# Second attention layer: other sequences of work in the VectorE and TensorE queues of one head

## The reference, cut to what matters

```python
scores = jnp.einsum('bhqd,bhkd->bhqk', q, k) / np.sqrt(DHEAD)      # 16 heads, 4 key heads, DHEAD 64
scores = jnp.where(causal_mask[None, None], NEG_INF, scores)
topk_vals, _ = jax.lax.top_k(scores, TOP_K)                        # TOP_K 64
threshold = topk_vals[..., -1:]
...                                                                # below the threshold: NEG_INF
                                                                   # softmax, times v, times Wo, added to x
```

## Time and profile before

| | |
|---|---|
| time, median of 3 runs | 2473.63 us (2472.95 to 2478.28) |
| the profiled execution, its own time | 2477.97 us |
| its span, first to last instruction | 2476.2 us |
| busy: PE, DVE, ACT, POOL | 77%, 67%, 57%, 23% of the span |
| mean granted TensorE clock | 0.872 |
| first and last cutoff of the changed stage (L1599, 32 of them) | start 1265.8 and 2445.0 us |

### The profile page before, as it was taken

How to read it: one execution, slowest core, us unless ns; L and a number is a source line. 1 busy time by engine, 2 the same in 40 slices (tenths; PEclk the granted TensorE clock), 3 DMA queues, 4 the chain that set the end, 5 groups by cost and what they waited for, 6 DMA issues and landing times. The chain is left out here.

```text
span 2476.2 us, 36312 instructions
## 1 busy us (share of the span) xinstructions
PE 1915.1 (77%) x10415; PEld 1113.4 (45%) x10448; DVE 1652.1 (67%) x3759; ACT 1400.3 (57%) x2883; POOL 573.0 (23%) x1478
## 2 busy tenths in 40 slices
PE   6678777799997896888567787777787847787776
PEld 3333333357775443555334444444444424444444
DVE  4566566621114465767488888888898878788874
ACT  2255555543331421323477877877778747877873
POOL 0011111100001440000233333333423423333340
PEclk7699999999995997999878888888977878888977
DMA  6000000010001220000200000100100000000000
GB/s 194 20 17 13 16 16 13 10 35 1 0 0 43 77 94 1 0 0 0 54 15 22 27 18 23 26 14 26 27 13 26 27 13 13 27 16 24 18 18 10
DMA packets 38262, 62.40 MB, mean 25 GB/s; under 512 B 10225, under 2 KB 15347, under 8 KB 38004
## 3 DMA queue, kind: packets, MB, share of 16 engines
q1 hardware_dynamic: 38069, 60.51, 8.3%
HBM read 34.14 MB, written 17.83 MB: 21 GB/s over the span
## 5 line engine op out<-in xcount | busy, mean ns | idle before, releaser
L1451 ACT ACTIVATE a_trash<-a_sc,a_search 128x1024 bf16<-128x1024 f32 (+7 forms) x768 | 585.6, 768 | 52.8 <-DVE a_sc L1560 20.2
L1262 PE MATMUL a_ps_o<-a_kT,a_v 128*65 128x512 f32 (+3 forms) x768 | 335.7, 542 | 128.2 <-DVE g_x L1616 113.6
L1229 PE MATMUL a_ps_s<-a_k,a_q 128*128 128x512 f32 (+3 forms) x768 | 323.4, 533 | 42.0 <-DVE a_sc L1560 28.3
L1246 PE MATMUL a_ps_t<-g_ident,a_sc 128*128 128x128 f32 x1152 | 276.5, 322 | 4.9 <-ACT a_short L1461 4.9
L1468 ACT ACTIVATE a_kT<-a_ps_t 128x512 f32<-128x512 f32 x288 | 169.1, 587 | 186.1 <-PE a_ps_t L1248 186.1
L1560 DVE TENSOR_SCALAR_CACHE_REDUCE a_sc<-a_ps_s,g_search 128x1024 f32<-128x1024 f32 (+7 forms) x256 | 208.3, 814 | 84.0 <-PE a_ps_s L1231 69.1
L479 DVE TENSOR_REDUCE a_top<-a_ps_row 128x1 f32<-128x512 f32 (+3 forms) x384 | 196.5, 553 | 93.9 <-PE a_ps_row L366 60.1
L1248 PE MATMUL a_ps_t<-a_minus,a_short 128*128 128x128 bf16 x1152 | 257.6, 248 | 0.0
L461 ACT ACTIVATE a_prob<-a_ps_col 128x1024 f32<-128x1024 f32 (+7 forms) x256 | 159.9, 653 | 156.2 <-PE a_ps_col L423 96.9
L1246 PEld LDWEIGHTS a_ps_t<-g_ident,a_sc 128*128 128x128 f32 x1152 | 193.9, 168 | 97.3 <-issue 66.5
L1534 DVE SCALAR_TENSOR_TENSOR a_below<-a_sc,a_found 128x640 f32<-128x640 f32 (+7 forms) x256 | 212.6, 841 | 0.0
(11 more groups left out here) (257 smaller groups left out, 3321.5 us busy)
## 6 DMA issues: line engine op xcount, KB each, us to landing
a_v<-g_v SPq DMA_DIRECT2D x32, 260.0 KB, 2.3
q1turned<-p_full SPq DMA_DIRECT2D x32, 256.0 KB, 2.0
a_q<-q1turned SPq DMA_DIRECT2D x32, 256.0 KB, 3.8
a_k<-k1turned SPq DMA_DIRECT2D x32, 256.0 KB, 4.3
stack<-p_parts SPq DMA_DIRECT2D x24, 256.0 KB, 3.8
a_q<-stack SPq DMA_DIRECT2D x32, 96.0 KB, 2.2
a_k<-stack SPq DMA_DIRECT2D x32, 96.0 KB, 2.2
le_w<-d_w SPq DMA_DIRECT2D x1, 2048.0 KB, 8.7
```

The source lines that it names most:

```text
L1229: pe.matmul(ps_s[:, j % 2, c:c + w], q[:, p, i * P:width], k[:, p, c:c + w], start=True, stop=True)
L1246: pe.matmul(out, columns(h, i)[:, c * P:(c + 1) * P], g.ident[:, :], is_transpose=True, start=True, stop=False)
L1262: m = pe.matmul(ps_o[0:VW1, lo // HALF, (lo % HALF) * P:CH], v[:, p, c, :], kT[:, u % 2, a * P:b * P], start=(c == 0), stop=(c == LAST[lo ...
L1451: act.activation(trash[:, u % 2, 0:(i + 1) * P], columns(h, i), ACT.Sign, scale=-1.0, bias=trials[:, p, c, i:i + 1], accum_out=balance[:, ...
```

## The change

PE's and DVE's sequences inside one section are written in another order. No operation is added or taken away, and POOL's and ACT's sequences stay. In PE's section the first `project` comes before scores 3 and the other seven behind it; scores 4 to 7 stand elsewhere among the turns and weighs; the late scores 0 come before turn 7, the late scores 1 behind weigh 7; the matmul on the verdict is the last of the section. In DVE's section `flags` comes ahead of the two reductions (now `find`), `judge` and `cut_off` ahead of the first `mark`, the parts of `shares` and `leave` are spread among marks and evacuations, the sorts have another order, and `keep_scores(6)` and `keep_scores(7)` are its last two instructions. `FINAL` becomes 0. The diff, with parts of the DVE sequence that only change the order of marks and sorts cut:

```diff
-        FIRST, FINAL = 4, 5
+        FIRST, FINAL = 4, 0
...
                     if ahead:
                         scores(n + 1, i2, p1, 2)
                     if leaving:
-                        for t in range(6):
-                            project(n - 3, t)
+                        project(n - 3, 0)
                     if ahead:
                         scores(n + 1, i2, p1, 3)
                     if leaving:
+                        project(n - 3, 1)
...
                         project(n - 3, 7)
                     if gating:
-                        turn(n - 2, h + 2, odd, 0)
+                        turn(n - 2, h + 2, odd + 0, 0)
+                    if ahead:
+                        scores(n + 1, i2, p1, 4)
+                    if gating:
                         turn(n - 2, h + 2, odd + 1, 1)
-                    for x in range(TU):
-                        if sorting and x == TU - 1:
-                            pe.wait_ge(verdict_ready, n)
-                            pe.matmul(ps_t[0:1, 1 - odd, 0:TB], g.ones[:, 0:1], verdict[:, :], start=True,
-                                      stop=True).then_inc(flag_back, 1)
-                        if gating:
-                            weigh(n - 2, i4 * 2 + h // 2 - 1, h % 2, odd + x, x)
-                            if x + 2 < TU:
-                                turn(n - 2, h + 2, odd + x, x + 2)
-                        if ahead and x in (0, 1, 3, 5):
-                            scores(n + 1, i2, p1, HALF + (x + 1) // 2)
-                        if late and x in (6, 7):
-                            scores(n + 2, i4 * 2 + (h + 2) // 2, 1 - p1, x - 6)
+                        turn(n - 2, h + 2, odd + 2, 2)
+                        weigh(*head, odd + 0, 0)
+                    if ahead:
+                        scores(n + 1, i2, p1, 5)
...
+                    if ahead:
+                        scores(n + 1, i2, p1, 7)
+                    if gating:
+                        weigh(*head, odd + 5, 5)
+                    if late:
+                        scores(n + 2, i4 * 2 + (h + 2) // 2, 1 - p1, 0)
+                    if gating:
+                        turn(n - 2, h + 2, odd + 7, 7)
+                        weigh(*head, odd + 6, 6)
+                        turn(n - 2, h + 2, odd + 8, 8)
+                        weigh(*head, odd + 7, 7)
+                    if late:
+                        scores(n + 2, i4 * 2 + (h + 2) // 2, 1 - p1, 1)
+                    if gating:
+                        weigh(*head, odd + 8, 8)
+                    if sorting:
+                        pe.wait_ge(verdict_ready, n)
+                        pe.matmul(ps_t[0:1, 1 - odd, 0:TB], g.ones[:, 0:1], verdict[:, :], start=True, stop=True).then_inc(flag_back, 1)
...
                     if ahead:
                         keep_scores(0)
                         keep_scores(1)
-                    if sorting:
-                        dve.wait_ge(sifted, n)
-                        dve.tensor_reduce(found[:, :], ...)
-                        dve.tensor_reduce(found2[:, :], ...)
                     if gating:
                         flagged = flags()
                     if sorting:
-                        mark(4)
+                        find()
                     if gating:
                         judge(flagged)
                         after(made[0])
                         cut_off()
                     if sorting:
-                        mark(3)
-                        mark(5)
+                        mark(4)
                     if leaving:
                         shares(0)
+                    if sorting:
+                        mark(6)
+                    if leaving:
+                        leave(0)
                         shares(1)
-                        leave(0)
-                        leave(1)
...
+                        sort(6, 2)
+                        sort(0, 2)
                     if ahead:
                         keep_scores(6)
-                    if sorting:
-                        sort(0, 2)
-                    if ahead:
                         keep_scores(7)
-                    if sorting:
-                        sort(5, 2)
```

More of the change, by code:

```diff
@@ L1285, in section @@
                         scores(0, 0, 0, 1)
+                    odd = h % 2
+                    head = (n - 2, i4 * 2 + h // 2 - 1, h % 2)
                     if ahead:
@@ L1293, in section @@
                     if leaving:
+                        project(n - 3, 1)
+                        project(n - 3, 2)
+                        project(n - 3, 3)
+                        project(n - 3, 4)
+                        project(n - 3, 5)
                         project(n - 3, 6)
                         project(n - 3, 7)
-                    odd = h % 2
                     if gating:
-                        turn(n - 2, h + 2, odd, 0)
+                        turn(n - 2, h + 2, odd + 0, 0)
@@ new lines, in section @@
+                    if ahead:
+                        scores(n + 1, i2, p1, 5)
+                    if gating:
+                        turn(n - 2, h + 2, odd + 3, 3)
+                        weigh(*head, odd + 1, 1)
+                        turn(n - 2, h + 2, odd + 4, 4)
+                        weigh(*head, odd + 2, 2)
+                        turn(n - 2, h + 2, odd + 5, 5)
+                    if ahead:
+                        scores(n + 1, i2, p1, 6)
+                    if gating:
+                        weigh(*head, odd + 3, 3)
+                        turn(n - 2, h + 2, odd + 6, 6)
+                        weigh(*head, odd + 4, 4)
@@ L1528, in section, with find @@
                     dve.sem_clear(step)
+                    def find():
+                        dve.wait_ge(sifted, n)
+                        dve.tensor_reduce(found[:, :], far.rearrange("p c s -> p s c"), AX.X, ALU.min).then_inc(found_ready, 1)
+                        dve.tensor_reduce(found2[:, :], low2.rearrange("p c s -> p s c"), AX.X, ALU.max).then_inc(found_ready, 1)
                     def mark(i):
@@ L1628, in section @@
                         keep_scores(1)
-                    if sorting:
-                        dve.wait_ge(sifted, n)
-                        dve.tensor_reduce(found[:, :], far.rearrange("p c s -> p s c"), AX.X, ALU.min).then_inc(found_ready, 1)
-                        dve.tensor_reduce(found2[:, :], low2.rearrange("p c s -> p s c"), AX.X, ALU.max).then_inc(found_ready, 1)
                     if gating:
@@ L1641, in section @@
                     if sorting:
-                        mark(3)
-                        mark(5)
+                        mark(4)
                     if leaving:
                         shares(0)
+                    if sorting:
+                        mark(6)
+                    if leaving:
+                        leave(0)
                         shares(1)
-                        leave(0)
-                        leave(1)
+                    if sorting:
+                        sort(4, 0)
                     if ahead:
                         keep_scores(2)
-                    if sorting:
[L1652 to L1658, removed]
                     if leaving:
                         shares(2)
-                        leave(2)
+                    if sorting:
+                        mark(0)
+                    if leaving:
+                        leave(1)
+                    if sorting:
+                        mark(7)
                     if ahead:
@@ L1664, in section @@
                     if sorting:
[L1665 to L1672, removed]
+                        sort(4, 1)
+                    if leaving:
+                        leave(2)
+                    if sorting:
+                        sort(0, 0)
+                        mark(3)
                     if ahead:
@@ L1675, in section @@
                     if sorting:
-                        sort(7, 1)
+                        mark(2)
+                        sort(3, 0)
+                        sort(6, 0)
+                        sort(3, 1)
+                        mark(1)
+                        mark(5)
+                        sort(7, 0)
                         sort(1, 0)
-                        sort(7, 2)
+                        sort(0, 1)
                         sort(1, 1)
-                        sort(6, 0)
-                        sort(5, 0)
                         sort(6, 1)
@@ L1685, in section @@
                     if sorting:
+                        sort(2, 0)
+                        sort(5, 0)
+                        sort(2, 1)
+                        sort(4, 2)
+                        sort(7, 1)
+                        sort(3, 2)
+                        sort(5, 1)
                         sort(1, 2)
-                        sort(0, 0)
-                        sort(5, 1)
-                        sort(0, 1)
+                        sort(7, 2)
+                        sort(2, 2)
+                        sort(5, 2)
```

(6 more changed lines are left out.)

## The result

The changed kernel takes 2642.69 us (median of 4 runs, 2640.41 to 2644.76), the kernel before 2475.95 us beside it. The ratio is 1.0675, with a 95% interval of 1.066 to 1.0689. The forecast was 2650 us.

A forecast was written before the change was run, and what follows sets the result against it. DVE was taken to set the pace, losing time only at the seam of two sections. A to E summed to +176 us; with the profiled 2477.97 us, less 4.3, that gave 2650 us, whole range 2575 to 2710 us.

The forecast's parts named there:

- A: At the seam, keep_scores(0) waits 1.88 us instead of 0.80, with only keep_scores(7) left as cover: +1.08 us a section.
- B: PE idles some 5 us ahead of the late scores 0, which then run at the 1.2 GHz level: +1.8 us.
- C: keep_scores(1) waits longer because turn 7, weigh 6 and turn 8 now stand between late scores 0 and 1: +2.27 us.
- rival 3: The slow clock lasts until the late scores 1 are done: 135 us more, 2785 us; chance 0.05.
- the stretch that the prediction leans on: The first stretch after a PE idle time in the trace before, where the clock came back while transposes ran.
- the rule on transposes: The Trainium skill's statement that transposes do not count as PE activity for the clock gate, keeping PE slow through the turns.
- D: At the branch, the mark leaves the shadow and two reductions go in: +0.9 us in each of 31 sections, 28 us.
- E: The verdict's matmul comes after weigh 8, at the end of PE's section: 0.1 us, at most 0.5; 3 us in all.
- what was costed at nothing: Spread of shares and leave, new places of scores 3 to 7, verdict's matmul leaving weigh 8's way, ACT's longer wait, loads.
- two kinds: DVE's waits before the change: 75.3 us ahead of the cutoff, and 40.3 us of keep_scores(0) and keep_scores(1) for PE.

The follow-up runs named there:

- Experiment three: The changed kernel with keep_scores(6) moved ahead of sort(7, 1) and keep_scores(7) behind it, PE's queue staying changed; 2492.66 us.
- Experiment six: The changed kernel with 4 extra matmuls over all 128 rows ahead of the late scores 0, where PE waits; 2583.38 us.
- Experiment four: The changed kernel with the late scores 1 directly behind the late scores 0, ahead of turn 7; 2688.7 us.
- experiments one: The kernel before with mark(4) moved behind cut_off, out of the shadow of the branch; 2504.74 us.
- nine: The kernel before with mark(3) and mark(5) also ahead of judge, so three marks lie in the branch's shadow instead of one; 2433.02 us.
- experiment eight: The changed kernel with one more wait on SP, so the loads of v, q and k start only after the next cutoff; 2626.92 us.
- experiment five: The changed kernel with 5 extra 512-wide matmuls over 65 rows ahead of the late scores 0, where PE waits; 2691.05 us.

## Why the prediction was right

The size and the reasons held: +167 us measured beside +176 forecast. By its own steps:

- **A, B and C together.** Forecast +5.15 us a section, measured 7.5 - 2.1 = +5.4 in VectorE's waits. Experiment three takes all of it away at once: 1.7 us of these waits are left a section, less than the 2.1 before.
- **A, the wait behind `keep_scores(6)`.** Held. The evacuation ends at about 1817.0 and PE starts the late scores at 1817.04.
- **B, the clock.** Held in kind and size: late scores 0 of 3.4 to 3.8 us in every steady section, 4.84 to 5.7 us of idle time ahead of them where "some 5" was forecast. Experiment six gives its worth as 59 us (forecast 50). What the step did not have is the first idle time, 2.3 us ahead of weigh 5: in most sections the clock was down before the wait that the step names. In the section shown the clock was back when the turns began, which take 0.28 and 0.22 us; in 19 of the 26 sections that can be read the first of them still took 0.31 to 0.42. The late scores 1 always took 1.67 us, so rival 3 falls. A turn is one transpose and one ordinary matmul in alternation, so neither these rows nor the stretch that the prediction leans on tests the rule on transposes by itself.
- **C, turns in the way of the late scores 1.** The sum was right and the place was wrong. The step said that `keep_scores(1)` would wait 3.4 us for the late scores 1, and `keep_scores(0)` 3.7 us for the late scores 0. They wait 0.9 and 5.7 to 7.1. I had left out a wait in the code: `keep_scores(0)` also waits on `t_ready` until turn 8 has read the score buffer. Turn 7, weigh 6 and turn 8 so hold up the first evacuation; the late scores 1 are made while it runs. In this order both accounts end `keep_scores(1)` at the same moment, which is why the time came out. Experiment four tells them apart, and the step as written fails it. That its sum fits all the same is luck of this order.
- **D, the branch.** Held, and shown both ways by experiments one (+28 us) and nine (-43 us). The mark took 0.89 us outside the shadow, not 1.05. In the short sections the gap is 3.4 to 3.6 us, as forecast. But on the mean it rose by 1.15 us, since it is 4.6 to 5.2 us in every other section; in the kernel before only about every fourth was long (up to 3.9 us). That lengthening was not in the prediction; experiment eight removes it and gives 16 us.
- **E and what was costed at nothing.** The flag's reduction (L1602) has no wait in VectorE's list from 1300 to 2450 us. ScalarE waits 7.75 us for turn 7 (forecast 7). It also waits for POOL's next trials (L1429) now, 96 us between 1300 and 2450 us; VectorE's list has no wait for the counts that hang behind them.

The waits at the seam and at the branch grew by 5.4 + 1.15 = 6.5 us a section together; the period grew by 5.86. Part of the difference is busy time. Over the same 27 periods of the kernel before VectorE was busy for 881.25 us, against 869.81 now, so 0.4 us a section less:

```profile
1301.50:2342.80 1041.30, 791.50 (x3942) 464.77 (x3942) 881.25 (x1966) 795.63 (x1809) 369.94 (x1134) 0.84 0.08 21
```

One reading of the prediction was too strong. It says that nearly all of DVE's idle time in the kernel before is of two kinds. In these 27 periods it is 160 us, of which they make up 122, about three quarters; the rest is 12.2 us ahead of evacuations (above) and smaller waits. No term of the sum hangs on it.

## What to carry to other kernels

Where engines hand a double-buffered tile to and fro, the producer's last work before a seam needs enough cover on the other engine for the whole way back; ask of each reordering what runs beneath that way, and read every wait of the instruction at its end, not only that for its input. The time of a data-dependent branch was free here for work that does not depend on it, so put work in front of it. And an idle time of PE can cost twice: once for the wait, once for the slow matmuls behind it.

## What the runs showed of the hardware

- PE's work between idle times did not bring the clock back alike. In eight sections of experiment five weigh 5 was slow nearly throughout (1.85 to 1.97 us) and the five 512-wide f32 matmuls over 65 rows behind it ran at the 1.2 GHz level through all of 8.74 us; in no section of that run did a clock that was down come back within them. In the sections of experiment six with as slow a weigh 5, four over 128 rows took 4.1 to 5.8 us and the clock was back at 2.4 GHz before they ended. The Trainium skill (TensorE: Matmul & The Clock Gate, Part 1) says that the clock depends on how busy PE has been recently; both kinds leave PE without gaps here, so time without gaps alone does not account for the difference. The two kinds also differ in their operands (a table of Wo, the constant v), so that the rows are the cause is not shown.
- A branch on a value that an engine has just written costs 3.7 to 4.0 us from the flag's reduction to the next instruction in the short sections of the changed kernel, and 4.9 to 5.5 in every second section, where the packet of code starts late among 0.77 MB of loads. With the loads out of the way the gap was 3.2 to 3.5 us in all steady sections.
